# Values placed on a block diagonal by DMA, residual rows added by an identity product in PSUM

## The reference, cut to what matters

```python
x = x + conv(_ln_c(x))          # conv: per column l, attention over the 32 positions n, 8 heads of 8 dims
    q, k, v = heads(z @ Wq), heads(z @ Wk), heads(z @ Wv)      # z = layer norm of the 64 dims
    g = sigmoid(heads(z @ Wg + bg))
    w = softmax(q k^T / sqrt(8) + bias)                        # (l, head, n, n)
    out = (g * (w v)) @ Wo + bo
t = tokens(x)                   # 2048 tokens of 256 numbers
x = t + ffn(_ln_t(t))           # router, top 2 of 8 experts, silu(gate) * up, down
```

## Time and profile before

| | |
|---|---|
| median of 3 runs | 356.41 us (354.51 to 356.92) |
| profiled execution | 355.87 us, of which its span is 354.1 us |
| busy in the span: PE, DVE, ACT, POOL | 294.2, 276.3, 209.4, 209.6 us |
| mean granted clock of PE | 0.918 of full speed |
| scores of attention step 1 start | 58.75 us |
| scores of attention step 7 start | 125.30 us |
| loop over expert blocks starts | about 180 us |

### The profile page before, as it was taken

One profiled execution on the slowest core, in us unless ns is written; L12 is line 12 of the kernel. 1 busy time (PEld: TensorE's weight loads), 2 busy tenths in 40 slices (PEclk: granted clock), 3 DMA queues, 4 the chain that ended last, 5 costly groups with the idle time before them and its releaser, 6 DMA issues.

```text
span 354.1 us, 11094 instructions
## 1 busy us (share of the span) xinstructions
PE 294.2 (83%) x3773; PEld 181.3 (51%) x3774; DVE 276.3 (78%) x569; ACT 209.4 (59%) x380; POOL 209.6 (59%) x178
## 2 busy tenths in 40 slices
PE   0497948878877867996899999999999999999970
PEld 0196534445544545332445656666666666666640
DVE  3988797878899998878748887887888788788750
ACT  0266789789999995368235455555555555555520
POOL 2833041775888889763330676667577585766462
PEclk9968995889999996995589999999999999999996
DMA  7450100254455555998324777767788677877652
GB/s 181 89 185 0 62 0 4 88 187 143 144 191 152 174 179 154 302 263 228 73 62 91 120 126 129 124 122 128 125 143 140 119 122 126 130 138 126 107 76 30
DMA packets 70464, 44.99 MB, mean 127 GB/s; under 512 B 47993, under 2 KB 63353, under 8 KB 70049
## 3 DMA queue, kind: packets, MB, share of 16 engines
q1 hardware_dynamic: 62080, 33.83, 37.8%
q0 software_dynamic: 7584, 10.65, 19.1%
q10 hardware_dynamic: 768, 0.14, 0.3%
HBM read 23.43 MB, written 9.63 MB: 93 GB/s over the span
## 4 chain that ended last, share of the span: by engine, by line
PE 53%; DVE 14%; ACT 9%; issue 9%; DMA 8%; POOL 4%; POOLq 1%; ACTq 0%; DVEq 0%
PE bank L857 23%; PE bank L880 10%; DMA out_dram<-z_two,gate 6%; ACT kq L1035 3%; PE bank L674 3%; PE bank L583 3%; DVE maxes L1322 2%; PE bank L845 2%; DVE s_exp L1331 2%; PE bank L757 2%; DVE e_t L1341 2%; PE bank L665 2%; PE bank L547 2%; DMA w_exp<-in_L_conv_pairs_dram 2%; ACT s_exp L1041 1%
## 5 line engine op out<-in xcount | busy, mean ns | idle before, releaser
L857 PE MATMUL bank<-w_exp,v_t 128*128 x468 | 114.0, 381 | 1.4 <-DVE v_t L1521 1.4
L529 POOL DMA_INDIRECT out_dram<-z_two,gate x39 | 66.5, 1706 | 51.0 <-ACT z_two L1156 38.1
L857 PEld LDWEIGHTS bank<-w_exp,v_t 128*128 128x128 f16 x468 | 45.9, 98 | 41.3 <-issue 3.3
L880 PE MATMUL bank<-w_exp,kq 128*128 x468 | 58.0, 273 | 0.9 <-DVE w_stage L1567 0.9
L517 POOL DMA_INDIRECT w_stage<-token_rows,gate x39 | 41.2, 1055 | 23.0 <-issue 8.8
L880 PEld LDWEIGHTS bank<-w_exp,kq 128*128 128x128 f16 x468 | 45.4, 98 | 15.2 <-issue 1.4
L1147 ACT ACTIVATE kq<-w_stage 128x512 f16<-128x512 f32 x38 | 23.9, 630 | 37.2 <-DVE w_stage L1550 37.2
L432 POOL TENSOR_TENSOR w_exp<-w_stage,w_exp 128x1024 f16<-128x1024 f32 x16 | 34.1, 2134 | 13.0 <-ACT w_exp L1046 13.0
L1557 DVE TENSOR_TENSOR kq<-w_stage,kq 128x512 f16<-128x512 f32 x38 | 26.3, 692 | 16.5 <-ACT kq L1147 16.5
L1542 DVE TENSOR_TENSOR kq<-bank,v_t 128x512 f32<-128x512 f32 x39 | 27.0, 691 | 8.2 <-PE bank L857 8.1
L1550 DVE TENSOR_TENSOR w_stage<-s_exp,kq 128x512 f32<-128x512 f32 x39 | 27.4, 701 | 4.5 <-DVE kq L1542 1.4
(11 more groups left out here) (256 smaller groups left out, 526.7 us busy)
## 6 DMA issues: line engine op xcount, KB each, us to landing
w_stage<-in_L_ffn_gate_w_dram SPq DMA_DIRECT2D x8, 512.0 KB, 3.6
w_stage<-in_L_ffn_up_w_dram SPq DMA_DIRECT2D x8, 512.0 KB, 3.6
w_stage<-in_L_ffn_down_w_dram SPq DMA_DIRECT2D x8, 512.0 KB, 3.6
x_rows<-in_x_dram SPq DMA_DIRECT2D x8, 256.0 KB, 6.2
out_dram<-x_rows SPq DMA_DIRECT2D x4, 512.0 KB, 6.5
v_t<-in_L_ffn_up_b_dram SPq DMA_DIRECT2D x2, 1024.0 KB, 10.5
token_rows<-z_stack SPq DMA_DIRECT2D x4, 512.0 KB, 6.5
z_two<-z_stack SPq DMA_DIRECT2D x6, 256.0 KB, 2.8
```

The source lines that it names most:

```text
L529: pool.indirect_dma_start(out, bass.IndirectOffsetOnAxis(t_scatter[:, b:b + 1], 0), yw[b % 2], None, compute_op=ALU.add).then_inc(s[f"y_la ...
L857: mm = pe.matmul(GU[par][k][:], xs[par][:, c, :], w_exp[:, w * W_EXP + k * W_PIECE + c * FF:][:, bass.ds(e, FF)], start=(n == 0), stop=(n ...
L880: mm = pe.matmul(YB[:, 0:L_COL], hs[par][:, c, :], w_exp[:, w * W_EXP + 2 * W_PIECE + c * L_COL:][:, bass.ds(e, L_COL)], start=(n == 0), s ...
```

## The change

The zeros and the diagonal of `v_tile` stay, but its layout becomes block, tile, head, number, so that one block is a contiguous 2,304 bytes of a partition. ACT writes the values of all 128 rows with one activation into a new buffer `v_row`, in which POOL has set the ones once (one memset where there were eight). SP then issues four DMAs a step, one for each block of 32 rows, that copy `v_row` onto the diagonal. PE waits for these DMAs before `attend`; ACT waits for them before it writes `v_row` again. The load of `gate_rows`, which now lies in `v_row`, moves from the start of SP's list to behind the last step. `add_rows` is taken from DVE. In `project_out` PE first multiplies the residual rows with an fp32 identity into bank 7, reading `x_rows` with the position innermost (a stride of 256 numbers), and the four projection products add to that; ACT then takes bank 7 out with the bias into `x_rows` (`rows_out`), in step j for step j-1, behind the exponentials of half 1. The last one stands in ACT's list behind the first four router copies. Small constants move from `pair_c` to `small`.

```diff
+            def place_values(j):
+                if j == 0:
+                    sp.wait_ge(s["ones_ready"], N_ONES)
+                if j >= 2:
+                    sp.wait_ge(s["av_ps"], 2 * (j - 1))
+                sp.wait_ge(s["v_copied"], j + 1)
+                for u in range(GROUP):
+                    rows = slice(32 * u, 32 * u + 32)
+                    sp.dma_start(v_tile[j % 2][rows, u], v_heads[rows]).then_inc(s["v_in"], 16)
...
+            place_values(0)
             for j in range(PAIRS - 1):
+                place_values(j + 1)
                 if j >= 1 and j + 3 < PAIRS:
                     copy_tokens(j + 3)
                 load_weights(j + 1)
+            sp.wait_ge(s["v_in"], 16 * GROUP * PAIRS)
+            sp.dma_start(gate_rows, gate_b).then_inc(s["rows_in"], 16)
...
-            for t in v_tile:
-                for u in range(4):
-                    ones(pool.memset(t[32 * u:32 * u + 32, :, :, u, D_HEAD], 1.0))
+            ones(pool.memset(v_heads[:, :, :, D_HEAD], 1.0))
...
                 if c == 0:
-                    pe.wait_ge(s["v_ready"], GROUP * (j + 1))
+                    pe.wait_ge(s["v_in"], 16 * GROUP * (j + 1))
...
                 pe.wait_ge(s["gated_ready"], j + 1)
+                cols = slice(PAIR * j, PAIR * (j + 1)) if isinstance(j, int) else bass.ds(j * PAIR, PAIR)
+                pe.matmul(bank[7], ident[:], x_rows[:, :, cols].rearrange("p n l -> p l n"), start=True, stop=False,
+                          skip_group_check=True)
...
-                                       turned[:, h], start=True, stop=True)
+                                       turned[:, h], start=False, stop=True, skip_group_check=True)
...
-                for u in range(GROUP):
-                    rows = slice(32 * u, 32 * u + 32)
-                    act.activation(v_tile[j % 2][rows, :, :, u, 0:D_HEAD],
-                                   bank[4][rows, :].rearrange("p (t h c) -> p t h c", t=8, h=HEADS),
-                                   ACT.Copy).then_inc(s["v_ready"], 1)
+                if j >= 1:
+                    act.wait_ge(s["v_in"], 16 * GROUP * j)
+                act.activation(v_heads[:, :, :, 0:D_HEAD], bank[4].rearrange("p (t h c) -> p t h c", t=8, h=HEADS),
+                               ACT.Copy).then_inc(s["v_copied"], 1)
...
+            def rows_out(j):
+                act.wait_ge(s["wo_ps"], j + 1)
+                act.activation(x_rows[:, :, PAIR * j:PAIR * (j + 1)], bank[7].rearrange("p (l n) -> p n l", l=PAIR),
+                               ACT.Identity, bias=bo_col).then_inc(s["x1_ready"], 1)
...
                 exps(j, 1)
+                if j >= 1:
+                    rows_out(j - 1)
                 weights_high(j, 0)
...
                 soften(j, 1)
-                if j >= 1:
-                    add_rows(j - 1)
                 turn(j, 1)
```

More of the change, by code:

```diff
@@ L92, in build @@
         tok_s = sb("tok_s", [P, 2, 4, 32])
-        pair_c = sb("pair_c", [P, 64])
+        pair_c = sb("pair_c", [P, 16])
         small_i = sb("small_i", [P, 2], i32)
-        gate_rows = sb("gate_rows", [EXPERTS, FF])
+        v_row = sb("v_row", [P, 8 * HEADS * VCOL])
+        v_heads = v_row[:].rearrange("p (t h c) -> p t h c", t=8, h=HEADS)
+        gate_rows = v_row[0:EXPERTS, 0:FF]
         maxes = sb("maxes", [P, 2, 2 * CHUNK])
@@ L134, in build @@
         wb_sb = pair_c[:, 2:10]
-        pair_mv = pair_c[:, 16:32].rearrange("p (j s) -> p j s", s=2)
-        pair_sd, pair_r, pair_t = (pair_c[:, 32 + 8 * i:40 + 8 * i] for i in range(3))
+        pair_mv = small[:, 112:128].rearrange("p (j s) -> p j s", s=2)
+        pair_sd, pair_r, pair_t = (small[:, 152 + 8 * i:160 + 8 * i] for i in range(3))
         eps_col, eps_tok = pair_c[:, 12:13], pair_c[:, 13:14]
@@ L144, in build @@
         g_col, b_col, bo_col, bg_col, qb_col, kb_col, vb_col, gb_col = (small[:, 144 + i:145 + i] for i in range(8))
-        v_tile = [v_t[:, i, :].rearrange("p (t h b c) -> p t h b c", t=8, h=HEADS, b=GROUP) for i in range(2)]
+        v_tile = [v_t[:, i, :].rearrange("p (b t h c) -> p b t h c", b=GROUP, t=8, h=HEADS) for i in range(2)]
         N_TABLES = 13
-        N_CONST, N_PAR, N_CENTER, N_ONES, N_PREP = 10, 18, 7, 2 + 2 * 4, 1 + 1 + 1 + 1 + 2
+        N_CONST, N_PAR, N_CENTER, N_ONES, N_PREP = 10, 18, 7, 3, 1 + 1 + 1 + 1 + 2
         var_col, sd_col, rs_col, tmp_col = (small[:, 32 + 16 * i:48 + 16 * i] for i in range(4))
@@ L251, in build @@
             q_ps k_ps v_ps g_ps s_ps av_ps at_ps wo_ps
-            q_ready k_ready max_ready sub_ready exp_ready et_ready v_ready
+            q_ready k_ready max_ready sub_ready exp_ready et_ready v_copied v_in
             rden_ready norm_ready gate_ready gate_one gated_ready x1_ready w_hi_done w_hi_pool w_lo_done
@@ L282, in _ @@
             sp.dma_start(rb_row, router_b.partition_broadcast(P)).then_inc(s["r_in"], 16)
-            sp.dma_start(gate_rows[:], gate_b).then_inc(s["rows_in"], 16)
             def load_weights(e):
@@ L626, in project @@
                 else:
-                    pe.wait_ge(s["v_ready"], GROUP * j)
+                    pe.wait_ge(s["v_copied"], j)
                     pe.wait_ge(s["gate_ready"], j)
@@ L691, in attend @@
                                        e_t[:, c, h // 4, P * q + 32 * (h % 4):P * q + 32 * (h % 4) + 32],
-                                       v_tile[par][:, 4 * c + q, h, :, :], start=True, stop=True)
+                                       v_tile[par][:, :, 4 * c + q, h, :], start=True, stop=True)
                 mm.then_inc(s["av_ps"], 1)
@@ L803, in gate_bias_rows @@
                         pe.wait_ge(s["gb_ready"], e - 4)
-                    pe.matmul(bank[GATE_BANK[e]], ident[0:EXPERTS, e:e + 1].broadcast_to([EXPERTS, P]), gate_rows[:],
+                    pe.matmul(bank[GATE_BANK[e]], ident[0:EXPERTS, e:e + 1].broadcast_to([EXPERTS, P]), gate_rows,
                               start=True, stop=True).then_inc(s["gb_ps"], 1)
@@ L1091, in _ @@
             act.activation(sd_tok[:, 1:2], eps_tok, ACT.Sqrt).then_inc(s["table_loaded"], 1)
+            rows_out(PAIRS - 1)
             tokens_out(1, 0)
@@ L1364, in apply_gate @@
                                          op0=ALU.add, op1=ALU.mult).then_inc(s["gated_ready"], 1)
[L1366 to L1371, removed]
             def dve_step(j):
@@ L1407, in _ @@
                 dve.bn_stats(bn2[:, n, 0:6], x_rows[:, n, head]).then_inc(s["stats_ready"], 1)
-            add_rows(PAIRS - 1)
             dve.wait_ge(s["x1_ready"], 1 + PAIRS)
```

## The result

Median of four runs after: 362.81 us (361.32 to 364.40); the kernel before, run beside it, 356.18 (354.51 to 356.92). The ratio is 1.0198, 95% interval 1.0153 to 1.0242: slower by about 2%. The profiled execution took 361.32 us, its span is 359.2; before, 355.87 and 354.1. So of some 6.6 us between the medians the two traces show 5.1 in their spans, and it is these 5.1 that can be followed.

A forecast was written before the change was run, and what follows sets the result against it. A loop through DVE and PE was taken as the bound, ACT merely full. Start -1.3, steps +2.5 and end +1.3 made +2.5 us: 358.4 profiled, 358.9 median; own range 357 to 361, 8-in-10 range 355 to 366.

The forecast's parts named there:

- What bounds the steps: Steady attention step: a loop through DVE (7.34 us) and PE (2.90), 10.24 in all, sets it; ACT is merely full.
- `add_rows` off DVE gives nothing: DVE, behind the second subtraction: removing 0.73 us only lengthens idle time from 0.47 to about 1.2 us; gain 0.
- Values and `rows_out` on ACT: ACT's step: values 0.68 us instead of 2.58, `rows_out` 0.7 more; 1.2 us less, bringing about 0.2 in one step.
- The identity at 0.95 us: Identity product on PE, between gate and scores: 0.95 us each (bounds 0.95 and 1.83), 0.44 slack; +2.5 up to last scores.
- the rival built on it: Strided read halves PE's rate: each identity product takes 1.83 us, 7.3 us more in all, 366 us; chance 0.27.
- The start, -1.3: Start of the kernel: one memset instead of eight gives -0.55 us, earlier first exponentials 0.75; together -1.3 us.
- The clock gain that I named as a rival: First scores and behind the last: PE's higher clock and ACT's relief bring more, 355.8 us; chance 0.11 for clock or ACT.
- The DMAs cost nothing: Four SP copies a step: issue and landing 3 to 5 us, with 6.7 us before `attend` needs the values; cost 0.
- The end, +1.3: Behind the last scores: +0.5 us (bounds 0 and 1.4) at PE's low clock, +0.8 for the last `project_out`; together +1.3.

The follow-up runs named there:

- experiment 3: Values part alone: the kernel after without the identity product and `rows_out`, with `add_rows` back on DVE; 352.55 us, ratio 0.9938 to the kernel before.
- experiment 1: The kernel after, its identity product reading 512 neighbouring numbers instead of numbers 1,024 bytes apart (wrong residual, same work); 356.49 us, ratio 1.0038.
- experiment 2: The kernel after, its identity product reading the residual in runs of 32 neighbours and writing PSUM with a 64-byte step, same sum; 356.34 us, ratio 1.0012.
- experiment 5: The kernel after, its identity product reading every second number of neighbouring residual vectors, a step of 8 bytes (wrong rows); 359.12 us in one execution.
- experiment 6: The kernel after, its identity product reading every fourth number of neighbouring residual vectors, a step of 16 bytes (wrong rows); 361.29 us in one execution.
- experiment 7: The kernel of experiment 3 with POOL's memset of ones done eight times in a row; 355.16 us, ratio 0.9986.
- experiment 8: The kernel of experiment 3 once more, unchanged, on the same chip as experiment 7; 353.17 us, ratio 0.9931.
- experiment 4: Rows part alone: the kernel before with the strided identity product and `rows_out` on ACT, values still by four activations; 362.99 us, ratio 1.0242.

## Why the prediction went as it did

1. **What bounds the steps: right.** The loop through DVE and PE, with ACT only full, is shown by experiment 3, and the chain after runs where the prediction put it.
2. **`add_rows` off DVE gives nothing: right.** DVE's idle time there went from 0.47 to 1.12 us; I wrote about 1.2.
3. **Values and `rows_out` on ACT: right.** 0.60 and 0.67 us, foreseen 0.68 and 0.7. The relief moved one score, by the 0.2 us foreseen: in experiment 3 the step whose scores had waited 0.55 us for keys went from 10.44 to 10.23 us, and its scores now follow DVE's subtraction.
4. **The identity at 0.95 us: this step failed.** It takes 1.90, a little over the upper of my two bounds, 1.83. I chose between the bounds by DVE's strided operand. That another engine reads with a stride at little loss says nothing of PE's read of a moving operand; the row was the nearest that I had and still no evidence, the less so since it sets a multiplication against a sum. (I wrote that no row shows PE reading with a stride. One does: at 169.15 the fp16 products of L819 read 39 numbers 64 bytes apart. But each of them follows a weight load of its own, so the row doesn't give the rate of the read.) The rule named beside it was, and the rival built on it had the mechanism: experiments 1, 2, 5 and 6. Worked out again with 1.90, a step whose scores followed DVE gets 1.90 - 0.44 = 1.46 longer; measured are 1.38, 1.44 and 1.40 in three of the four, and 0.86 and 1.21 in the two whose scores waited for keys, where some 1.2 was due.
   The rival's price was too high: 7.8 up to the last scores, measured 5.82. The fourth, from the scores of 2 to those of 3, got shorter by 0.47. In it PE pauses inside `attend` for nothing that the profile shows, and the pause went from 2.50 to 1.27 us:

```profile
73.72 0.28 PE L704 MATMUL bank<-v_t,e_t 128*32 128x36 f32 x9 [1.27 <-issue]
```

   What this pause is, and why it shrinks, stays open.
5. **The start, -1.3: right in sign, a third of its size.** Of the 3.85 us, experiments 7 and 8 give about 2 to POOL's memsets by the medians, and 2.63 by their two traces; I had 0.55, the wait alone. A single trace is a weak witness here: the seven kernels with one memset start their scores of step 1 anywhere from 54.75 to 56.54, and the kernel after, at 54.90, is near the early end. What is left by the traces, 58.75 - 57.38 = 1.37, goes to the values' path, since the rows alone (experiment 4) leave the start where it was; I had 0.75. The clock gain that I named as a rival did come in this trace, but in centring, not where I placed it: the bias part of the first scores still takes 1.82 us, against 1.88.
6. **The DMAs cost nothing: right.** SP takes 2.42 us to issue the four and each lands after 2.0; a row of SP's timeline and one of the page:

```profile
117.31 2.42 SPq L318 DMA_DIRECT2D v_t<-v_row  x4
```

```profile
v_t<-v_row SPq DMA_DIRECT2D x32, 72.0 KB, 2.0
```

   The last is in at about 117.31 + 2.42 + 2.0 = 121.7; `attend` starts at 126.56 and follows PE's own order. 4.8 us to spare, of 6.7 expected.
7. **The end, +1.3: too small.** Measured +3.20. The last identity takes 1.88, not 0.95: from the last transposes to the last projection it is 4.25 us, 2.53 before, so 1.72 more; I had 0.8 for that place. Nearly all of the rest, 1.42, lies between the identity of step 6 and DVE's small copy, where I took 0.5 (of 0 to 1.4). From the start of that identity to the end of the copy it is 145.34 - 135.35 = 9.99 us; before it was 8.57, from the earlier trace rows's `project_out` at 133.25 to a copy that ended at 141.82. Up to the start of the copy it is 7.86 us against 7.36, just the 0.5 that I took; the other 0.92 is the copy's own length, 2.13 against 1.21. In both kernels the copy ends with the second of POOL's two products (after: 141.09 + 4.22 = 145.31); before:

```profile
137.57 4.22 POOL L432 TENSOR_TENSOR w_exp<-w_stage,w_exp 128x1024 f16<-128x1024 f32 x2 [0.24 <-ACT w_exp L1046]
...
140.61 1.21 DVE L1399 COPY maxes<-small 128x16 f32<-128x16 f32 x1
```

   In the kernel after these products start late because ACT first waits 0.73 us for the projection, writes `rows_out`, and only then converts the weights for which POOL waits 2.79. So a wait put on ACT reached DVE by way of POOL. Whether that costs anything hangs on a tenth of a microsecond. In experiment 6, with the same lists and nearly the same waits (ACT 0.70, POOL 2.65 us), the copy starts just before the first product ends, and is done at once:

```profile
141.49 4.22 POOL L446 TENSOR_TENSOR w_exp<-w_stage,w_exp 128x1024 f16<-128x1024 f32 x2 [2.65 <-ACT w_exp L1057]
...
143.49 0.17 DVE L1410 COPY maxes<-small 128x16 f32<-128x16 f32 x1
```

   From the start of the identity to the end of the copy it is then 143.66 - 135.78 = 7.88 us, less than the 8.57 before, and the whole end comes out at 29.24 us, +1.04. In the kernel after the copy starts at 143.21, where the first product ends (141.09 + 2.11 = 143.20), and lasts until the second ends. So some 2 of the 3.20 us hang on a near miss in the one execution that was profiled. Without it my +1.3 would have looked right, though the last identity costs twice what I gave it.

**The sum again.** For the profiled execution I had 358.4; plus 3.3 for the steps and 1.9 for the end, less 2.55 for the start, that is 361.05, and it took 361.32. So close a sum is partly luck: what follows the cast took 200.6 us before and 200.5 after, but anything from 199.4 to 200.8 in the seven kernels that compute the same result. Two misses of opposite sign kept the time between my forecast and its first rival: the median of 362.81 is above the forecast's own 357 to 361, and the wide range holds it only because it reached to the full price of the strided read.

## What to carry to other kernels

Before an fp32 product is added to a loop through PE, look at how many neighbours of its moving operand lie in 16 bytes: if it is one, turn the pattern round so that PSUM is written with the stride and SBUF is read in runs. An engine that is 98% busy may still have nothing to give; only the wait that ends last tells. Where an instruction of one engine may have to wait for the end of another engine's, a tenth of a microsecond can decide over two, so what one trace shows there is not yet a price. A change with two halves is run as two: here one is worth -0.6% and was hidden under the other's +2.4%.

## What the runs showed of the hardware

- In the steps, at a granted clock of 1.00 (2.4 GHz), an fp32 product of 512 columns takes 1.05 us if it reads neighbours, 1.09 with two numbers in 16 bytes, and 1.90 to 1.97 with one. Behind the steps, at the same clock, it takes 0.95 (experiment 1, at 144.24) and 1.81 (after, at 150.38).
- At 1.2 GHz the strided read costs hardly more: the identity row at 135.35, in a stretch at a granted clock of 0.50 (1.2 GHz), takes 2.08 us, against 1.97 at the high one. With reads in runs the same place (experiment 2, also at 0.50) shows 2.08 too. So half the read rate and half the clock do not add up.
- A copy of 16 numbers a partition on DVE took 1.21 us before, 2.13 after and 0.48 in experiment 4, each time until a product of POOL's ended. In all ten traces, where it took from 0.17 to 2.13 us, its end and that of a POOL product lie within 0.12 us of each other. In experiment 4 it started in the last half microsecond of POOL's first product, and ended with it (144.76 + 2.11 = 146.87):

```profile
144.76 4.22 POOL L432 TENSOR_TENSOR w_exp<-w_stage,w_exp 128x1024 f16<-128x1024 f32 x2 [2.25 <-ACT w_exp L1049]
...
146.43 0.48 DVE L1402 COPY maxes<-small 128x16 f32<-128x16 f32 x1
```

  That fits the pair of SBUF ports that DVE and POOL hold in turns for a whole instruction (the Trainium skill, "SBUF — State Buffer", section "Terms"); no run here took POOL's products away to prove it. The spans of experiments 3 and 4, -3.1 and +6.4 us, make +3.3, and the kernel after has +5.1; of the 1.8 left over some 0.9 lies in the end, where this copy is, and the rest is spread over the other stretches.
